# Attention maxima in pairs: two neighbouring PSUM banks and one VectorE maximum instruction for four heads

## The reference

```python
Qh = Q.reshape(b, nq, h, hd).transpose(0, 2, 1, 3)
energy = jnp.einsum('bhqd,bhkd->bhqk', Qh, Kh) / scale      # layer 0: 154 + 64 keys
attention = jax.nn.softmax(energy, axis=-1)                 # the maximum over the keys
x = jnp.einsum('bhqk,bhkd->bhqd', attention, Vh)
...
scores = jnp.einsum("bhsd,bhtd->bhst", q, k) * scale        # layer 1: 154 keys
attn = jax.nn.softmax(scores, axis=-1)
```

## Time and profile before

| | |
|---|---|
| median of 3 runs | 1012.13 us (1011.17 to 1013.39) |
| the profiled execution | 1012.16 us, of which its span (first to last instruction) 1010.4 us |
| TensorE matmul busy | 912.1 us, 90% |
| VectorE busy | 581.9 us, 58%; of it the maxima (L1327) 180.4 us in 384 instructions |
| ScalarE, GpSimd busy | 432.4 us (43%), 283.9 us (28%) |
| mean granted TensorE clock | 0.955 of full speed |

### The profile page before, as it was taken

The page is one execution under the profiler, slowest core; times in us unless marked ns, Lnnn a source line. Parts: engine busy times, 40 slices in busy tenths (PEclk is TensorE's granted clock), DMA queues, the critical chain, the costliest instruction groups (busy, mean ns, idle before and its releaser), DMA issues. The chain is left out here.

```text
span 1010.4 us, 15438 instructions
## 1 busy us (share of the span) xinstructions
PE 912.1 (90%) x5522; PEld 648.1 (64%) x5522; DVE 581.9 (58%) x1403; ACT 432.4 (43%) x795; POOL 283.9 (28%) x404
## 2 busy tenths in 40 slices
PE   2689999999999898999989799998999999999776
PEld 2555446465555444888877545545888878888665
DVE  3665757675757574455556367674536454354477
ACT  1345555667654555233332356655223232222330
POOL 7411514545644532010211055332001010010243
PEclk9989989999979799999999889999999999999995
DMA  6000000000010210000000211100000000000001
GB/s 153 4 2 14 1 15 2 15 2 18 19 53 2 76 36 9 14 1 1 1 1 1 77 29 37 44 24 13 2 1 1 1 1 1 1 1 1 1 1 42
DMA packets 27573, 18.10 MB, mean 18 GB/s; under 512 B 6221, under 2 KB 25770, under 8 KB 27370
## 3 DMA queue, kind: packets, MB, share of 16 engines
q1 hardware_dynamic: 27498, 17.12, 6.1%
HBM read 15.63 MB, written 1.05 MB: 17 GB/s over the span
## 5 line engine op out<-in xcount | busy, mean ns | idle before, releaser
L1327 DVE TENSOR_REDUCE mneg<-PS 128x2 f32<-128x308 f32 (+1 forms) x384 | 180.4, 515 | 115.5 <-PE PS L880 114.7
L1490 DVE TENSOR_TENSOR work<-PS,work 128x512 f32<-128x512 f32 (+2 forms) x168 | 114.8, 685 | 169.3 <-PE PS L1065 126.1
L1796 ACT ACTIVATE work<-PS 128x512 f32<-128x512 f32 (+2 forms) x168 | 99.8, 596 | 245.9 <-PE PS L1065 232.1
L1773 ACT ACTIVATE work<-PS 124x512 f32<-124x512 f32 (+1 forms) x272 | 156.8, 601 | 92.8 <-PE PS L1000 91.9
L1079 PEld LDWEIGHTS PS<-down_w,work 128*128 128x128 f32 (+2 forms) x1344 | 157.8, 191 | 5.7 <-DVE work L1490 1.3
L1079 PE MATMUL PS<-down_w,work 128*128 128x128 f32 (+2 forms) x1344 | 158.3, 275 | 1.0 <-DVE work L1490 1.0
L1063 PE MATMUL PS<-xh_sb,arena 128*128 128x512 f32 (+2 forms) x336 | 138.0, 411 | 9.6 <-DVE work L1490 9.6
L1065 PE MATMUL PS<-xh_sb,arena 128*128 128x512 f32 (+2 forms) x336 | 132.6, 395 | 0.0
L1064 PE MATMUL PS<-xl_sb,arena 128*128 128x512 f32 (+2 forms) x336 | 132.0, 393 | 0.0
L1867 POOL TENSOR_SCALAR rstd<-bn_mv 128x4 f32<-128x4 f32 x32 | 7.3, 227 | 436.2 <-DVE bn_mv L1225 436.1
L880 PEld LDWEIGHTS PS<-kb_sb,qxt_sb 97*128 97x128 f32 x256 | 45.4, 197 | 63.5 <-issue 33.8
(11 more groups left out here) (183 smaller groups left out, 1277.4 us busy)
## 6 DMA issues: line engine op xcount, KB each, us to landing
ctx_rep<-in_ctxT SPq DMA_DIRECT2D x12, 308.0 KB, 3.2
stage<-in_w SPq DMA_DIRECT2D x8, 256.0 KB, 4.2
stage<-in_wg SPq DMA_DIRECT2D x8, 176.0 KB, 2.4
stage<-in_wu SPq DMA_DIRECT2D x8, 176.0 KB, 2.4
x_res<-in_x SPq DMA_DIRECT2D x4, 256.0 KB, 3.9
down_w<-in_w SPq DMA_DIRECT2D x1, 1024.0 KB
down_w<-in_wd SPq DMA_DIRECT2D x8, 128.0 KB
out<-x_res SPq DMA_DIRECT2D x4, 256.0 KB, 2.3
```

The costliest lines, as they stand in the source:

```text
L1327: dve.tensor_reduce(mneg[:, a % 2, t, h0:h0 + 2], PS[:, bank_of["mx", a, m], 0:2 * (KT0 if layer == 0 else KC)].rearrange("p (h n) -> p h ...
L1490: dve.tensor_tensor(HH[0:rows, e % 2, j, :], PS[0:rows, 2 * (n % 2) + 1, :], SS[0:rows, n % 2, :], ALU.mult).then_inc(*sig["h"].mark((i, n)))
L1773: act.activation(p_tile(i, n)[0:rows, :], PS[0:rows, n % 2, :], ACT.Exp, scale=SCALE).then_inc(*sig["p"].mark((i, n)))
L1796: act.activation(SS[0:rows, n % 2, :], PS[0:rows, bank, :], ACT.Silu).then_inc(*sig["act"].mark((i, n)))
```

## The change

Both values of `f` go into two neighbouring banks, and one VectorE instruction takes the maxima of all four heads. So there are 16 steps for each attention in place of 32, each with two matmuls, one signal and one reduction over two banks. TensorE's matmuls are as many as before, each with its own weight load. A step takes a pair of banks, waits for both, and both are free again when the one reduction is done. The numbers in the opening, at which the value blocks and their masks are interleaved, are halved. The plans spread 16 steps over the same slots by the same formula.

```diff
-N_MAX = 2 * G * T
-MT_LAST = 2 * T
+N_MAX = G * T
+MT_LAST = T
...
             def scores_for_max(i_main, a, m):
 
-                g, f, t, layer = m // (2 * T), m // T % 2, m % T, a // B
-                bank = take_bank(i_main, ("mx", a, m))
-                if m % (2 * T) == 0:
+                g, t, layer = m // T, m % T, a // B
+                bank = take_bank(i_main, ("mx", a, m), pair=True)
+                if t == 0:
                     pe.wait_ge(*sig["qxt"].at((a, g)))
...
                 wait_for(bank)
+                wait_for(bank + 1)
                 w = 2 * (KT0 if layer == 0 else KC)
-                pe.matmul(PS[:, bank, 0:w], QXT[0:KX_ROWS, a % 2, g, t * 128:(t + 1) * 128],
-                          KB(layer)[0:KX_ROWS, a % 2, g, f * w:(f + 1) * w], start=True, stop=True).then_inc(*sig["mx_psum"].mark((a, m)))
-                taken[bank] = sig["mx"].at((a, m))
+                for f in range(2):
+                    mm = pe.matmul(PS[:, bank + f, 0:w], QXT[0:KX_ROWS, a % 2, g, t * 128:(t + 1) * 128],
+                                   KB(layer)[0:KX_ROWS, a % 2, g, f * w:(f + 1) * w], start=True, stop=True)
+                mm.then_inc(*sig["mx_psum"].mark((a, m)))
+                taken[bank] = taken[bank + 1] = sig["mx"].at((a, m))
...
-                if m == 8:
+                if m == 4:
                     v_blocks(None, 0, 0)
-                if m == 20:
+                if m == 10:
                     v_blocks(None, 0, 1)
-                if m == N_MAX - 5:
+                if m == N_MAX - 3:
                     maxima_transposed(None, 0, 0)
...
             def maxima(i_main, a, m):
-                g, f, t, layer = m // (2 * T), m // T % 2, m % T, a // B
+                g, t, layer = m // T, m % T, a // B
                 dve.wait_ge(*sig["mx_psum"].at((a, m)))
...
-                h0 = g * HL + 2 * f
-                dve.tensor_reduce(mneg[:, a % 2, t, h0:h0 + 2],
-                                  PS[:, bank_of["mx", a, m], 0:2 * (KT0 if layer == 0 else KC)].rearrange("p (h n) -> p h n", h=2),
+                bank = bank_of["mx", a, m]
+                dve.tensor_reduce(mneg[:, a % 2, t, g * HL:(g + 1) * HL].rearrange("p (f h) -> p f h", f=2),
+                                  PS[:, bank:bank + 2, 0:2 * (KT0 if layer == 0 else KC)].rearrange("p f (h n) -> p f h n", h=2),
                                   AX.X, ALU.max, negate=True).then_inc(*sig["mx"].mark((a, m)))
```

More of the change, by code:

```diff
@@ L1601, in _ @@
                 maxima(None, 0, m)
-                if m == 13:
+                if m == 6:
                     v_mask(0, 0)
-                if m == 25:
+                if m == 12:
                     v_mask(0, 1)
```

## The result

The changed kernel took **1028.1 us** (median of 4 runs, 1023.9 to 1030.2) against 1012.8 for the kernel before beside it: ratio 1.0145, 95% interval 1.0113 to 1.0177. Run again later beside more runs of before (1014.0) it took 1027.4, ratio 1.0113 (1.0067 to 1.016). It is slower, as forecast, but by 12 to 15 us and not by 4: 1028 lies outside the predicted range, which ended at 1021.5.

What follows compares the result with a forecast made beforehand. TensorE, busy 90% of the span, was taken as the bound outside the opening, so its stalls are added to the end. Losses of 9.9 us less gains of 5.9 gave +4.0 on 1012.16, forecast 1016.2 us, range 1006.5 to 1021.5.

Steps and rivals of the forecast that it cites:

- the returning pair: Attention items: after a single user, maxima return to the pair just filled; reuse after 1.48 us, stall 0.42 in layers 1, 2.
- The paired reductions: VectorE: one reduction over two banks takes 0.800 us (616 columns) or 1.07 (872), 0.98 when overlapping its neighbour.
- forecast busy time of 555: VectorE's busy time over the whole kernel falls by 192 x 0.14 = 27 us to about 555.
- The standing still of layer 0: Layer 0's attention items: maxima wait for returning pairs behind x transposes, q and in slots 3 and 4; 3.1 us lost.
- the low-rank matmuls: Three items: low-rank matmuls wait for a whole pair where they waited for one bank; +0.3 us each.
- The opening: Opening, where VectorE works almost without a break: 16 pairs at 0.06 us each give -1.0 us.
- losses of 4.0 and 0.7 us: Layers 1 and 2: returning pairs cost 4.0 us; value blocks in slot 20 of two items +0.35 each.
- gains of 4.2 and 0.7: Last maxima moved from slot 21 to 20 in four items, -4.2 us; shorter VectorE queues at some ten places, -0.7.
- the last feed-forward item: Layer 1's last feed-forward item: one pair replaces two shared banks, standing still 8.2 us against 7.0, loss 1.2.
- rival (c): Whole kernel: much slower, through TensorE's granted clock; chance 0.16.

Runs made afterwards that it cites:

- moved places alone: Kernel before, single maxima and single banks, but each two maxima stand in the slot where the paired version has its pair; 1011.3 us, ratio 0.9989.
- two reductions: Changed kernel with the same pairs of banks, but two reductions for each pair, each bank released on its own; 1020.3 us, ratio 1.0048.
- forced alternation: Changed kernel, but behind a k projection or transposed maxima the next maxima take the pair holding that single user; 1036.3 us, ratio 1.0234.
- late release: Changed kernel with two reductions for each pair, each started behind its own matmul, both banks released by the second; 1025.3 us, ratio 1.0116.
- late start: Changed kernel with two reductions for each pair, both started behind the second matmul, each bank released by its own; 1024.6 us, ratio 1.0108.

## Why the prediction was wrong

**Right.** The direction, the mechanism of the returning pair, and its price. The paired reductions take 0.795 and 1.06 us (0.800 and 1.07 forecast), chained 0.97 (0.98). VectorE ended 14 us above the forecast busy time of 555: the 27 us subtracted whole durations, the rows show chained ones, and the maxima group fell by 14.1. That is 0.073 us for each of the 192 instructions saved, so as they are chained here only some half of the 0.14 by durations can be had. The returning pair needs 1.53 us where 1.48 was said. The standing still of layer 0, 3.1 us and 0.9 for the low-rank matmuls, shows as 4.0 in the profile (5.4, 1.3 either way, over the executions with layer 0 paired alone). The opening gained 1.1 to 1.9 us by the profiles, 1.0 forecast.

**The step that failed most: the balance in the items of layers 1 and 2.** The forecast set losses of 4.0 and 0.7 us against gains of 4.2 and 0.7, which is about nothing. The rest there rose by 7.4 us in the profiles (each known to 1), and with only these paired that of the whole kernel by 5.2 (1.7 either way). The places were counted nearly right: ten behind k and the transposed maxima, where nine were forecast, and one behind x transposes (634.54 in item 9, 1.54 us behind the pair before, where it was 1.26). At 0.47 for each of the ten, 0.28 for that one and 0.62 of idle time at each of the two value blocks they come to 6.2 us, for 4.7. What is left of the rise says that hardly any of the gain of 4.2 us arrived. With the moved places alone it is open how much of it comes (1 us by time, -4 to +2; 2.9 by the rest), and 1.7 us of the wait moved to the low-rank matmuls ahead of one of the transposes. I counted the idle time ahead of the transpose as if nothing else there was waiting for VectorE too. The term was also some 0.4 us too large as it was read: from the start of the last matmul I took off only 0.14 us, but without any wait a transpose starts 0.38 us behind a pair (647.13 to 647.51), which is 0.24 behind a single one. Two releases give back 6 us of the 7.4.

**The second: the last feed-forward item**, +1.2 us. It costs 2.8 (59.3 to 62.1 us, clock 1.00). The walk through its slots with one pair found less than half of it. 1.5 us are left with two reductions, and the moved places alone cost 0.1 (59.4 us), so some 1.4 belong to the one pair in place of two banks. The ratio of the run, 0.9985, does not show it.

**The third: the clock was left out of the sum.** It stood only as rival (c), at 0.16. Layer 0 got 17.7 us more at the lower level, some 8.9 us of time, and the same in the second profile and with layer 0 paired alone (0.91 each). The term "low-rank matmuls of three items wait for a whole pair ... (+0.3 each)" named the right place with the right stall (0.26 us more in item 2: 0.74 to 1.00) but left out the 0.53 us ahead of it and what comes behind: with 0.8 us more of standing still there, item 2 took 4.0 us more and item 3 3.3. The run with the low-rank products three slots later gives 7.7 us back in these two items, at a clock of 1.00. Over the whole kernel, though, less than this is left: the clock's part of the changed kernel is 1.9 us above before (3.9 either way), and 0.7 in the two profiled executions. So of the 12 to 15 us some 12 are standing still, where the sum had 4.0, and rival (c), much slower, came nearest to what was measured but not in its reason, the granted clock.

**Open.** How the 7.8 us of rest between two reductions and one divide is known only roughly (3.8 for the late release and 2.3 for the late start, each known to some 3 us; 0.7 and 0.5 in the feed-forward item). What the granted clock answers to is not shown: in item 2 of layer 0 it fell with waits of 0.53 and 1.00 us 1.6 us apart, it did not with 0.53 and 0.89 us 5.5 us apart nor with one of 0.74 us, and it did with three of 0.24 to 0.38 us over 6 us.

## What to carry to other kernels

The merged instruction saved 0.07 us of VectorE for each pair, but it released both banks only at its end and started only when both were full (0.7 and 0.5 us in the last feed-forward item); where another engine waits for those buffers, that can cost more than is saved, as here, and the two effects should be tried apart (same buffers, two instructions). Split every loss into standing still and granted clock, by stretch and over the whole kernel: here layer 0 lost 8.9 us by its clock, other items had less of it, and a part of the change (the feed-forward item) cost 2.8 us that the times of its run did not show. Take the split over many executions where they are on record, as the clock's part of a kernel moves by several us from one to the next. Where an instruction is merged, do it only in stretches where its own engine is the bound, here the opening.

## What the hardware showed that I had not expected

Chained VectorE reductions from PSUM overlap (seven of 1.06 us took 6.89 us in the opening), so that merging two into one saves only 0.07 us (166.3 against 180.4 us for 192 pairs, half of the difference of isolated durations, 0.14). The granted clock of layer 0 is reproducible to the item (0.92, 0.85, 0.94 and 0.93 in items 0 to 3 in both profiles of the changed kernel, and 0.91 over layer 0 also with layer 0 paired alone and with forced alternation), and a difference of under 1 us in TensorE's standing still goes with 6.5 us more at the lower level (item 2: clock 1.00 to 0.94, 2 x 0.06 x 54.1 us). VectorE's 2.84 us instruction in item 1 (2.87 before) is the largest single term in slot 20, and I had read it as ordinary work; it lies beside a GpSimd chain without a gap, and moving that chain would be the next thing to try.
